# A Mamba block and a mixture of experts on one core: the last batch row goes densely through all experts, and the end of every engine's order is written out

## What is computed

```python
h = layernorm(x) * (1 + ca) + sa
x = x + ga * mamba2(h)        # projection, 4-tap convolution, scan over 512 steps, gated norm, projection
h = layernorm(x) * (1 + cb) + sb
x = x + gb * moe(h)
# moe: logits = h @ Wg.T; the two greatest of 8 experts, softmax over the two;
#      expert e: (silu(h @ W1[e].T + b1[e]) * (h @ W2[e].T + b2[e])) @ W3[e].T + b3[e], hidden size 256
#      out = sum over the two chosen experts of weight * expert(h)
```

## Time and profile before

| | us |
|---|---|
| median of 3 runs | 832.32 |
| lowest, highest | 821.59, 838.61 |
| profiled execution, its time | 832.36 |
| its span, first to last instruction | 830.5 |
| TensorE, VectorE, ScalarE, POOL busy | 680.6, 559.4, 516.8, 462.0 |

### The profile page before, as it was taken

One profiled execution on the slowest core, in us unless ns is written; L12 is line 12 of the kernel. 1 busy time (PEld: TensorE's weight loads), 2 busy tenths in 40 slices (PEclk: granted clock), 3 DMA queues, 4 the chain that ended last, 5 costly groups with the idle time before them and its releaser, 6 DMA issues. The chain is left out here.

```text
span 830.5 us, 13734 instructions
## 1 busy us (share of the span) xinstructions
PE 680.6 (82%) x3713; PEld 518.9 (62%) x3713; DVE 559.4 (67%) x1640; ACT 516.8 (62%) x1223; POOL 462.0 (56%) x366
## 2 busy tenths in 40 slices
PE   3678899789789999998999999999966952774982
PEld 3246557556567776876787777768755731553662
DVE  2827967988986997898689978987743561231421
ACT  3784795896796899687969977886522310221320
POOL 2003004444453378757775786688687477357775
PEclk9779798999998999999999999999996967897997
DMA  5100001112013465455346444653645774857973
GB/s 186 28 0 1 1 27 32 45 52 71 33 58 102 119 168 129 105 155 125 92 105 174 107 97 103 204 104 90 180 107 120 200 204 95 202 123 149 191 169 28
DMA packets 81275, 88.86 MB, mean 107 GB/s; under 512 B 7360, under 2 KB 67696, under 8 KB 81200
## 3 DMA queue, kind: packets, MB, share of 16 engines
q1 hardware_dynamic: 54528, 61.37, 25.6%
q0 software_dynamic: 26672, 26.62, 18.0%
HBM read 54.50 MB, written 33.46 MB: 106 GB/s over the span
## 5 line engine op out<-in xcount | busy, mean ns | idle before, releaser
L457 POOL DMA_INDIRECT out<-xs x142 | 226.8, 1597 | 116.9 <-issue 53.2
L427 POOL DMA_INDIRECT rows<-payload,pos x128 | 131.6, 1028 | 68.2 <-issue 30.2
L880 DVE SCALAR_TENSOR_TENSOR xbc<-T,table,xbc 128x511 f32<-128x511 f32 (+2 forms) x192 | 141.9, 746 | 7.7 <-ACT xbc L599 3.1
L1133 DVE SCALAR_TENSOR_TENSOR xs<-FX,xs 128x128 f32<-128x128 f32 x142 | 43.1, 345 | 122.6 <-PE FX L1457 104.7
L1457 PE MATMUL FX<-wt,hid 128*128 128x128 f32 x568 | 87.8, 301 | 17.2 <-DVE hid L1125 17.2
L655 ACT ACTIVATE xt<-FX 128x256 f32<-128x256 f32 x71 | 27.0, 380 | 110.1 <-PE FX L1434 96.0
L1457 PEld LDWEIGHTS FX<-wt,hid 128*128 128x128 f32 x568 | 73.7, 203 | 26.6 <-DVE hid L1125 17.9
L648 ACT ACTIVATE sg<-FG,wt 128x256 f32<-128x256 f32 x142 | 59.3, 471 | 47.0 <-PE FG L1444 38.4
L1444 PE MATMUL FG<-xt,wt 128*128 128x256 f32 x284 | 77.6, 397 | 12.1 <-DMA wt<-in_wt 8.1
L1287 PE MATMUL T<-h,win 128*128 128x512 f32 x128 | 76.7, 698 | 12.4 <-DVE xbc L880 10.6
L1444 PE MATMUL FV<-xt,wt 128*128 128x256 f32 x284 | 78.2, 400 | 0.0
(11 more groups left out here) (207 smaller groups left out, 1343.5 us busy)
## 6 DMA issues: line engine op xcount, KB each, us to landing
wt<-in_wt SPq DMA_DIRECT2D x71, 386.0 KB
xs<-rows SPq DMA_DIRECT2D x71, 258.0 KB
x<-in_x SPq DMA_DIRECT2D x8, 512.0 KB, 4.3
out<-x SPq DMA_DIRECT2D x8, 512.0 KB
out<-xs POOLq DMA_INDIRECT x142
rows<-pad SPq DMA_DIRECT2D x8, 258.0 KB
rows<-payload,pos POOLq DMA_INDIRECT x128
gate_a<-gates SPq DMA_DIRECT2D x8, 128.0 KB, 4.3
```

Source lines behind the costliest of these rows:

```text
L427: pool.indirect_dma_start(d["rows"], bass.IndirectOffsetOnAxis(ap=pos[:, k, n:n + 1], axis=0), payload[:, n, :], None).then_inc(scattered, 16)
L457: pool.indirect_dma_start(d["out"], bass.IndirectOffsetOnAxis(ap=xs[:, t % XSR, c, PAY - 1:PAY].bitcast(U32), axis=0), xs[:, t % XSR, c, 0 ...
L880: last = nc.vector.scalar_tensor_tensor(out=xbc[:, t, k, tap:L], in0=T[:, k, 0:L - tap], scalar=w, in1=xbc[:, t, k, tap:L], op0=ALU.mult, ...
```

## The change

Pair 7's second batch row (512 tokens) is no longer sorted. Its h2, which lies on chip, goes through all eight experts, in ND = 16 dense units of 256 tokens; each result is multiplied by the token's share of that expert (zero for the six not chosen) and summed in `acc`, a part of `xn`. One product with the gate and one sum put it into x, and one store writes it. The expert weights for that lie in `mda` (five) and `decay` (three), loaded once pair 7 no longer needs these.

Pair 7 therefore scatters 8 times instead of 16 (only q = 0, 1, 4, 5), NTILES falls to 67 and LAST to 18; tiles 49 to 66 are listed last. A list UNITS holds tiles and dense units in one sequence of 83: two dense units ahead of each of tiles 42 to 46, one ahead of 47 and 48, four ahead of 49. From tile 42 on the turn goes to bank YB, and the down product of odd units to YA. The periodic orders of all engines are replaced by others, whose loops end earlier; after them each engine's calls are written out with numbers.

```diff
-NTILES = NP * PT + LAG
+DT = L // TR
+NTILES = NP * PT - L * 2 // TR + LAG
...
+def units():
+    seq, n = [("tile", t) for t in range(OPEN + 1)], 0
+    for t in range(OPEN + 1, NTILES):
+        for n in range(n, min(n + (2 if t < NTILES - LAST - 2 else 1 if t < NTILES - LAST else ND), ND)):
+            seq.append(("dense", n))
+            n += 1
+        seq.append(("tile", t))
+    return seq
...
+            def load_dense_weights(part):
+                if part == 0:
+                    sp_.wait_ge(seg_psum, J * NP)
+                else:
+                    sp_.wait_ge(ya_psum, C * NP)
+                for e in (range(EA), range(EA, E))[part]:
+                    sp_.dma_start(wd[e], d["wt"][e, :, :]).then_inc(wd_in[part], 16)
...
+            load_rows(32)
+            store_x1(6)
+            load_weights(33)
+            load_dense_weights(0)
+            load_rows(33)
...
+            load_weights(45)
+            load_dense_weights(1)
+            load_rows(45)
+            load_weights(46)
+            load_rows(46)
+            load_rows(47)
+            set_pads()
+            load_rows(48)
...
+            scatter(6, 2)
+            scatter(6, 3)
+            add_out(34)
+            second_weight(6)
+            scatter(6, 4)
+            scatter(6, 5)
+            scatter(6, 6)
+            power_y(7)
+            scatter(6, 7)
+            add_out(35)
+            power_norm2(7)
+            add_out(36)
+            add_out(37)
+            add_out(38)
+            add_out(39)
+            scatter(7, 0)
+            add_out(40)
+            scatter(7, 1)
+            add_out(41)
+            add_out(42)
+            add_out(43)
+            second_weight(7)
+            add_out(44)
+            scatter(7, 4)
+            add_out(45)
+            scatter(7, 5)
+            add_out(46)
...
-                nc.vector.tensor_tensor(out=hots[:, :, :], in0=hot[:, 0, :, :], in1=hot[:, 1, :, :], op=ALU.add).then_inc(hots_ready, 1)
+                n = J if p < NP - 1 else JS
+                if n < J:
+                    nc.vector.tensor_tensor(out=hots[:, n:J, :], in0=hot[:, 0, n:J, :], in1=hot[:, 0, n:J, :], op=ALU.subtract)
+                nc.vector.tensor_tensor(out=hots[:, 0:n, :], in0=hot[:, 0, 0:n, :], in1=hot[:, 1, 0:n, :], op=ALU.add).then_inc(hots_ready, 1)
...
+            def dense_shares():
+                vec.wait_ge(tanh_ready, NP)
+                for k, sign in ((0, 0.5), (1, -0.5)):
+                    last = nc.vector.tensor_scalar(topf[:, k, JS:J], tanh[:, JS:J], sign, 0.5, ALU.mult, ALU.add)
+                link(last)
+                for k in range(2):
+                    last = nc.vector.tensor_tensor(out=share[:, k, :, :], in0=hot[:, k, JS:J, :], in1=wide(topf[:, k, JS:J], E), op=ALU.mult)
+                link(last)
+                link(nc.vector.tensor_tensor(out=share[:, 0, :, :], in0=share[:, 0, :, :], in1=share[:, 1, :, :], op=ALU.add))
...
+                    else:
+                        e, j = n // DT, n % DT * 2 + c
+                        if e == 0:
+                            last = nc.vector.tensor_scalar(acc[:, j, :], got, share[:, 0, j, e:e + 1], None, ALU.mult)
+                        else:
+                            last = nc.vector.scalar_tensor_tensor(out=acc[:, j, :], in0=got, scalar=share[:, 0, j, e:e + 1],
+                                                                  in1=acc[:, j, :], op0=ALU.mult, op1=ALU.add)
...
+            def dense_result():
+                p = NP - 1
+                vec.wait_ge(gate_b_in[p % 2], 16 * (p // 2 + 1))
+                vec.wait_ge(ro_ready, UNITS.index(("dense", ND - 1)) + 1)
+                link(nc.vector.tensor_tensor(out=acc, in0=acc, in1=gate_b[:, p % 2, 1, :].unsqueeze(1).to_broadcast([P, JS, D]), op=ALU.mult))
+                vec.wait_ge(xn2_ready, NP)
+                nc.vector.tensor_tensor(out=x[:, p % XR, JS:J, :], in0=x[:, p % XR, JS:J, :], in1=acc, op=ALU.add).then_inc(dense_out, 1)
...
+                    wait_dense(pe, n)
+                    pe.wait_ge(h2_ready, NP)
+                    w, src = wd[n // DT], h2[:, L + n % DT * TR:L + (n % DT + 1) * TR]
...
+            turn_norm2(7)
+            expert_up(41, 0)
+            expert_up(41, 1)
+            expert_down(40)
+            logits(7)
+            expert_up(42, 0)
+            expert_turn(42)
+            expert_up(42, 1)
+            expert_down(41)
+            expert_up(43, 0)
+            expert_up(43, 1)
+            expert_down(42)
+            expert_up(44, 0)
+            expert_up(44, 1)
+            ranks(7)
+            expert_down(43)
+            expert_up(45, 0)
+            expert_up(45, 1)
+            turn_h2(7)
```

More of the change, by code:

```diff
@@ L50 @@
 LAST = NTILES - (PT * (NP - 1) - LAG)
+JS = J // 2
+ND = E * DT
+OPEN = PT * (NP - 2) - LAG
+AHEAD = 2
+EA = C * 2 * NH * P // WT
+def units():
[6 more added lines that the diff above has]
+    return seq
+UNITS = units()
+UNIT_OF = {v: u for u, (k, v) in enumerate(UNITS) if k == "tile"}
 TABLE = (("ident", P), ("upto", P), ("after", P), ("before", P), ("expo", J), ("experts", E), ("conv_w", NCT * KC),
@@ new lines, in _ @@
+            weight_by_dt(7, 0)
+            weight_by_decay(7, 0)
+            power_norm2(6)
+            add_out(29)
+            weight_by_dt(7, 1)
+            weight_by_decay(7, 1)
+            weight_by_dt(7, 2)
+            add_out(30)
+            weight_by_decay(7, 2)
+            add_out(31)
+            weight_by_dt(7, 3)
+            add_out(32)
+            scatter(6, 0)
+            scatter(6, 1)
+            add_out(33)
+            scatter(6, 2)
+            scatter(6, 3)
+            add_out(34)
@@ L511, in _ @@
+            add_out(63)
+            add_out(64)
+            add_out(65)
+            add_out(66)
         @block.scalar
@@ new lines, in _ @@
+            softplus_exponent(7)
+            mix_chunk(6, 3)
+            expert_hidden(23)
+            next_state(6, 0)
+            expert_out(22)
+            y_chunk(6, 0)
+            next_state(6, 1)
+            expert_out(23)
+            expert_hidden(24)
+            conv_taps(7, 0)
+            take_logits(5)
+            conv_taps(7, 1)
+            top_two(5)
+            which_two(5)
+            next_state(6, 2)
+            expert_out(24)
+            y_chunk(6, 1)
+            rows(5)
@@ new lines, in _ @@
+            expert_hidden(32)
+            next_state(7, 1)
+            expert_out(32)
+            take_logits(6)
+            top_two(6)
+            next_state(7, 2)
+            which_two(6)
+            mix_chunk(7, 3)
+            expert_hidden(33)
+            rows(6)
+            expert_out(33)
+            expert_hidden(34)
+            y_chunk(7, 2)
+            expert_out(34)
+            expert_hidden(35)
+            expert_out(35)
+            y_chunk(7, 3)
+            expert_hidden(36)
@@ new lines, in _ @@
+            expert_hidden(42)
+            expert_out(41)
+            expert_hidden(43)
+            which_two(7)
+            dense_shares()
+            expert_out(42)
+            expert_hidden(44)
+            rows(7)
+            expert_out(43)
+            expert_hidden(45)
+            new_tiles(7)
+            expert_hidden(46)
+            expert_out(44)
+            expert_out(45)
+            expert_hidden(47)
+            expert_out(46)
+            expert_hidden(48)
+            expert_hidden(49)
@@ new lines, in _ @@
+            to_tokens(7, 2)
+            intra(7, 0)
+            to_tokens(7, 3)
+            expert_down(30)
+            inter(7, 1)
+            intra(7, 1)
+            expert_up(32, 0)
+            expert_up(32, 1)
+            expert_down(31)
+            turn_norm2(6)
+            expert_turn(33)
+            new_state(7, 1)
+            expert_down(32)
+            logits(6)
+            expert_up(33, 0)
+            expert_turn(34)
+            new_state(7, 2)
+            turn_h2(6)
```

1303 lines of the change are left out of this document (980 added, 323 removed).

## The result

| | changed kernel, us | before, us, same chip | ratio, 95% interval |
|---|---|---|---|
| first comparison | 852.8 (849.6 to 854.0, 4 runs) | 827.8 (821.6 to 838.6, 4 runs) | 1.032 (1.027 to 1.038) |
| control in set 2 | 843.4 (4 runs) | 826.9 | 1.018 (1.014 to 1.022) |
| control in set 3 | 845.4 (6 runs) | 828.7 | 1.019 (1.016 to 1.023) |
| control in set 4 | 832.7 (6 runs) | 825.1 | 1.012 (1.007 to 1.016) |

A control is the changed kernel, unaltered, run again beside the variants of a set. The forecast was 817, with a range from 797 to 836. The changed kernel is slower in each of four comparisons, by 1.2 to 3.2 per cent; the forecast had the wrong sign. The profiled execution took 849.64 us with a span of 847.7, where before it was 832.36 and 830.5.

A forecast was written before the change was run, and what follows sets the result against it. POOL's chain of adds, each waiting for an earlier landing, was taken to bound the last 230 us. Tile 49 at 736, plus 77.0, plus 7.8, less 5, gave 815.8; with 1.9 around it 817.7, said as 817, range 797 to 836.

The forecast's parts named there:

- Part 5: New periodic orders on all engines: remove TensorE's waits or make new ones, between -15 and +15 us, taken as -5.
- The prediction's own sign: TensorE at 97% or more from 280 to 600, with as many products done, would show the periodic orders neutral.
- The start of the sum: Add times of the profiled execution before, 832.36 us with a span of 830.5; tile 49 was at 729.3 there.
- Part 1: Tail behind tile 49: four tiles less, so 17 gaps in 77.0 us (75.5 to 78.4) instead of 21 in 93.3.
- Part 2: POOL up to tile 49: bunched scatters start add 35 10.2 us later, 14 gaps then take 109; costs 7.
- landing alone: POOL's adds up to tile 49: gaps where only the landing is waited for, 7.9 to 8.3 us; 7.8 taken.
- Part 3: Sixteen dense units on TensorE ahead of tile 49: 48.5 us, wholly hidden beside the chain of landings.
- the cover of 9 us: At tile 49: TensorE's result leaves at about 727, before its add on POOL at 736.
- Part 4: Eight more weight loads on SyncE's queue: the first five end about 570, hidden; if not, some 10 us once.
- D: Rival, slower: TensorE bounds behind pair 7's normalisation, from 3.6 us a unit; 853 us; sign: adds await vector results; chance 0.14.
- C: Rival, no difference: gaps of 8.4 put tile 49 at 745, periodic orders give nothing; 831 us; chance 0.19.
- B: Rival, faster: periodic orders take 15 off, landings shorter until TensorE's 727 sets tile 49; 798 us; chance 0.23.

The follow-up runs named there:

- e8: Changed kernel with the periodic orders of the kernel before on all engines up to pair 5's second norm; 838.7 us, ratio 1.010.
- e5: Changed kernel with old orders to pair 7's residual, pair 6's scatters spread, pair 7's two adds later, SyncE's last loads in TensorE's order; 835.9 us.
- e6: Kernel before, with only SyncE's loads behind tile 49 in the order in which TensorE asks for them; 823.8 us, ratio 0.996.
- e9: Changed kernel with only SyncE's loads behind tile 49's in TensorE's order, the same kernel as e3, beside a control; 843.7 us, ratio 1.017.
- e11: Changed kernel without the products, activations and sums of its 16 dense units, weights still loaded, beside a control; 826.5 us, ratio 1.003.
- e13: The kernel of e5 without the dense units' work; 815.0 us, ratio 0.990.
- e7: Changed kernel with the first five dense weight loads moved behind load_rows(40), about 60 us later; 848.2 us.
- after: Changed kernel, unaltered, in the first comparison; 852.8 us, ratio 1.032, its profiled execution 849.64 us.
- c_after: Changed kernel, unaltered, run again as the control of the second set; 843.4 us, ratio 1.018.
- c_after2: Changed kernel, unaltered, run again as the control of the third set; 845.4 us, ratio 1.019.
- c_after3: Changed kernel, unaltered, run again as the control of the fourth set; 832.7 us, ratio 1.012.
- e3: Changed kernel with only SyncE's loads behind load_rows(49) in the order in which TensorE asks for them, no control in its set; 829.3 us, ratio 1.005.
- e4: Changed kernel without the dense units' products, activations and sums, weights still loaded, no control in its set; 825.9 us, ratio 0.999.
- e12: Changed kernel with old periodic orders to pair 5, the end's loads in TensorE's order and no dense units' work; 816.6 us, ratio 0.990.
- e14: The kernel of e5 with eight dense units ahead of tiles 42 to 49 and the other eight among tiles 50 to 62; 819.6 us, ratio 0.993.

## Why the prediction was wrong, point by point

**Part 5, the periodic orders: the step that failed first.** Priced at -5 with bounds of -15 and +15, measured at +11.3 ahead of add 34 in the first profile: inside the bounds, and not the value taken. The waits that it started from the earlier trace rows did shrink, from 7.9 us in seven to 3.8 in two, and others took their place in the same window:

```profile
PE T L1868 <- DVE xbc L1240: 7.0, 7, 1.7
PE FX L2016 <- DVE xs L1512: 6.7, 6, 1.4
PE YA L1895 <- ACT decay L824: 6.1, 4, 4.1
PE S L2005 <- DVE state L1280: 3.8, 2, 1.9
```

The prediction's own sign, TensorE at 97 per cent from 280 to 600, came out at 95.1. Putting the old loops back (e8) took 6.6 us off by the medians, 3.0 by the profiles, so that much of the loss is shown to be theirs; the rest of the 11.3 is open. Old orders up to pair 7 brought its residual 21 us forward in the second set (e5, 616.5 against 637.5), but with the dense units ahead of tile 49 only 9.6 of that arrived there. The choice of a gain had no row behind it: a wait that an order takes away was read, what the new order makes wait was not.

The start of the sum was also high by luck of the profile. It goes from an execution of 832.4 us, where the kernel before has medians of 824 to 829, and e6, whose order is the same up to tile 49, has add 34 at 603.9 instead of 609.4. From a typical execution the same sum would have come out some 5 us lower, and further from the result.

**Part 1, the end: the second step, mis-sized.** 77.0 us for 17 gaps, measured 92.1. The mean price of 4.44 us a gap was carried over. It doesn't carry: before, the last four gaps cost 3.7, 3.7, 6.1 and 3.7, and the first 17 came to 76.1. In the changed kernel the last gaps alternate between 3.7 and about 6. With the loads in order POOL still waited 26.8 us for landings in the 17 gaps (e9), where the kernel before waited 11.2 us in 21. That an add must wait for the tile before it more often because each expert has fewer tiles left would fit this; no run shows it. With the loads in order the 17 gaps took 85.5 to 87.6 us, where the first 17 of the kernel before with its loads in order (e6) took 72.2. So some 9 to 11 us of the 15 are the price of the gaps, which no variant took back, and 4 to 6 go with the order of SyncE's loads. The chain of waits of the changed kernel shows the queue at work:

```profile
774.18 3.96 DMA wt<-in_wt
778.18 2.07 PE FG L2033 x4
780.25 0.32 PE FX L2046
780.57 2.02 PE FX L2053 x8
...
784.63 3.68 DMA xs<-rows
788.35 0.69 PE YB L2016 x2
```

Weights 58 stood on SyncE behind rows 59, which wait until the adds of tile 52 have landed; TensorE wanted the weights and waited. Then rows 60 stood behind `load_weights(60)`, which waits for a down product of TensorE. So a load that TensorE needs waits on SyncE for a landing, and the next for TensorE itself, and adds 57 and 59 came after gaps of 10.3 and 8.8 us. The prediction had looked at SyncE's queue for the dense loads and the pads only, not for the new order of the end.

**Part 2, POOL's burst.** Add 34 to 35 took 19.3 us against 17.4 forecast: the step is right. The 109 us to tile 49 were met too (108.5), but not for the reason given: without the dense units it was 97.5 us (e11), 7.0 a gap, and the dense units filled up the rest, 8.55 us of it ahead of tile 49 itself. The Trainium skill (DMA: Bandwidth & Descriptors, Anatomy of one DMA) had given 5.6 us a gap as an estimate; of the 280 gaps between adds 35 and 49 in all profiles the least is 5.77 and the middle one 7.35, so no trace reaches it, and the 7.9 to 8.3 taken for "landing alone" lay above the middle.

**Part 3, the dense units: called hidden, and they were not.** Priced at nothing. Taken out, they gave 6.2 us in the changed kernel (e11) and, in e5's order, moved tile 49 from about 119 us behind the residual to 98 (e13). The products cost what was said; TensorE's timeline shows 0.9 to 1.2 us for each part of a unit:

```profile
658.45 1.11 PE L2033 MATMUL FG<-h,mda 128*128 128x256 f32 x4
...
659.61 1.03 PE L2033 MATMUL FV<-h,mda 128*128 128x256 f32 x4
```

But logits end at 658.4 instead of the assumed 646 to 650, since pair 7 itself was late, and the 24 units from there to 747 took 3.69 us each instead of 3.03 and 3.40. TensorE was busy 82.2 of the 89 us from 658 to 747, at clock 0.96, so it was all but full: the products, the ranks and the turn back left 6.8 us idle. That puts tile 49's result at 747 where 727 had been reckoned: the cover of 9 us ahead of the add was not there.

**Part 4, the weights.** Right: five loads issued at 572.4 to 574.8, rows of tile 33 at 575.63 (before 576.48), and moving the loads away brought nothing (e7).

**The rivals.** D, slower by TensorE behind pair 7, had 0.14 and 853 us. Its mechanism is half of the truth: it was to decide from 3.6 us a unit, and 3.69 were measured up to tile 49, where the add waits for a vector result, as D's sign said. Its number, 853, was met by another sum: beyond tile 49 the time went to SyncE's queue and the turns, not to TensorE's units, and ahead of pair 7 to the orders. C had the orders at nothing and tile 49 at 745: the place was right, the way to it wasn't. B's shorter landings do exist, 97.5 us for the 14 gaps in e11 where B had 100, but only without the dense units' work, and its periodic orders went the other way.

**Not settled.** How the changed kernel's medians of 832.7 to 852.8 us come about, where those of the kernel before lie between 824 and 829. The profiles differ from pair 5 on, ahead of all that the end does: pair 7's residual came at 634 to 641 us in after, c_after, c_after2 and e9, and at 620 to 621 in c_after3 and e3, whose profiles are both of their fastest run. The same kernel without the dense work took 825.9 and 826.5 us on two chips (e4 and e11), so it doesn't show this spread; why isn't known. How much the new orders cost ahead of the end therefore isn't one number: 21 us at that residual in the second set, 3.5 in the third for the loops alone, none in the fourth (620.2 against 621.3 in e12). And the single parts (6.6 for the loops, 2 to 4 for the loads, 6 for the dense work) are medians of different chips; e12, with all three, was 16.1 below its control, which is about their sum.

## What to carry to other kernels

Work put in place of an engine's idle time is hidden only if it ends before the result that the other engine waits for: reckon when the first piece can start if the stage before it is late, and what else the engine must do until the last one ends. Then put it where both engines have slack; here the dense units at other places, eight of sixteen behind tile 49, made 0.9 per cent worse into 0.7 per cent better. And where a queue is written out by hand, each load that waits for a buffer holds all behind it: write it in the order of need.

## What the runs showed of the chip that was not expected

- The work behind a wait ran slowly as well. In the changed kernel TensorE was granted 1.00 from 758 to 776 us, 0.50 from 778 to 790 and 0.87 from 790 to 796: four products of an up half took 1.03 us at the 2.4 GHz level, and after waits the last of which was 2.63 us for weights four such took 2.07, which is the 1.2 GHz level, later 1.52 and then 1.03 again:

```profile
774.30 1.03 PE L2033 MATMUL FV<-xt,wt 128*128 128x256 f32 x4
...
778.18 2.07 PE L2033 MATMUL FG<-xt,wt 128*128 128x256 f32 x4 [2.63 <-DMA wt<-in_wt]
...
790.54 1.52 PE L2033 MATMUL FG<-xt,wt 128*128 128x256 f32 x4
...
793.20 1.03 PE L2033 MATMUL FV<-xt,wt 128*128 128x256 f32 x4
```

- More work went with a higher granted clock: with the dense units it was 0.88 from 728 to 821 us, without them 0.76, and e14's end ran at 0.99. Whether this repaid any of the added work is not shown.
- One program's medians differ by 20 us between comparisons where those of another, of nearly the same work, differ by 5. A variant without a control in its own set could not be read: e3 seemed to bring 14 us and brought about 2.
